# DLRM tower: six small GpSimd writes between rows of five gathers, from tile 7 on, in place of a wait for a landing

## The chip, the cores and the metric

The kernel runs on one core of a Trainium2 chip. The metric is the device time of one execution in microseconds (us), the median of several runs. The core's engines are TensorE (PE in the profile; its weight loads are PEld), VectorE (DVE), ScalarE (ACT), GpSimd (POOL) and SyncE (SP). Each has its own stream of instructions, and they are kept in step by semaphores only.

## The reference

A small recommendation model is applied to a batch of 2048 rows. For each row, 32 table lookups give 32 vectors of 16 numbers; every pair of them is multiplied and summed (496 pairs); these sums and 16 dense numbers go through three matrix layers.

```python
e = jnp.stack([tbl_0[ids[:, 0]], ..., tbl_31[ids[:, 31]]], axis=1)      # 2048 x 32 x 16
row, col = _pair_indices(32)
z = jnp.sum(e[:, row, :] * e[:, col, :], axis=2)                        # 2048 x 496
h = jnp.concatenate([z, dense_ctx], axis=1)                             # 2048 x 512
h = jnp.maximum(h @ W_top1 + b_top1, 0.0)                               # 512 x 512
h = jnp.maximum(h @ W_top2 + b_top2, 0.0)                               # 512 x 256
y = h @ W_top3                                                          # 256 x 1
```

## The kernel before

The batch is cut into 16 tiles of 128 rows, one row to a partition. Of the 32 fields, 17 have small tables (1250 or 1000 rows), which PE looks up with matmuls (`look_up`, L633). The other 15 fields have large tables and are gathered by GpSimd: one indirect DMA for each field and tile fetches 128 table rows of 64 bytes into `emb` (L367), 240 in all. The 15 fields of a tile come in three groups of 7, 5 and 3 fields.

GpSimd's program is a plain list of these gathers, tile after tile. Ahead of a group in tile t it waits until VectorE has used the group of tile t - 2 (L358). After every fifth field of a tile (`place % RUN == RUN - 1`, places 4, 9 and 14) it waits until the gather that it has just issued has landed (L373), so that the gathers go out in rows of five with a pause between rows. The last tile has no such wait: its 15 gathers, which start from 352.11 to 369.59 us, follow each other without a pause.

VectorE multiplies the groups with the fields before them as soon as a group has landed (L489, L498, L508), sums part of the pairs itself (L517), and picks the looked-up rows (L470). ScalarE copies operands into PSUM (L868, L875), the pair sums into SBUF (`copy_z`, L882), and does the layers' relus (L888, L893). PE sums the other pairs by 16 transposing matmuls for each 128 pairs (`sum_chunk`, L663; `turn`, L670, for the chunk that VectorE summed), and does the layers (L683, L692, L699). PE tells the others that it is done by a semaphore update on the last matmul of such a group (`summed`, `h1_ready`, `h2_ready`, `looked`). The engines run one or two tiles behind each other, so that a tile's layers are done while the next tile's gathers go out.

The last tile is written out by hand. Its fields are waited for in five pieces (`LAST_PIECES`, three and two fields of group 1, and then one field each of group 2). After the last field: `piece(4)`, `last_group_inside`, a sum (L517), then on PE `turn` (L670), a copy on ScalarE (L981), a quarter of layer 1 (L780), relus (L994, L607), layer 2 (L803), relus (L997, L610), layer 3 (L811), a copy (L899) and the store (L335). ScalarE's order in the last tile is `copy_group(t, 0)`, then `relu1(t - 1, 2)` and `relu1(t - 1, 3)`, then `copy_end(0, 2)`, `copy_group(t, 1)` and so on.

Of the kernel before, what the change touches and what calls it, by code (L numbers as in the profile page):

```python
# [5 lines left out]
P = 128  # L6
# [20 lines left out]
LARGE = [f for f in range(F) if f not in SMALL]  # L27
# [17 lines left out]
SUB = 16  # L45
# [7 lines left out]
GROUPS = [7, 5, 3]  # L53
GROUP_AT = [S + sum(GROUPS[:g]) for g in range(len(GROUPS) + 1)]

RUN = 5

SHIFTS = (S - 1) // 2
CIRCLES = [(GROUPS[0] - 1) // 2, (GROUPS[1] - 1) // 2, 0]
# [55 lines left out]
def dlrm_tower(nc, dense, ids, small_ids, ids_dram, tables, w1, b1, w2, b2, w3, out):  # L115
    with ExitStack() as ctx:
        def sb(name, shape, dt=F32):
            return ctx.enter_context(nc.sbuf_tensor(name, shape, dt))

        def sem(name):  # L120
            return ctx.enter_context(nc.semaphore(name))
# [16 lines left out]
        row_ten = sb("row_ten", [P, 1])  # L138
        one = sb("one", [P, 1])
        scrap = sb("scrap", [P, 1])  # L140
        cand_int = sb("cand_int", [P, SLOTS], I32)
        field_int = sb("field_int", [P, TENS, SLOTS], I32)
        place_int = sb("place_int", [P, TENS * SLOTS], I32)
# [39 lines left out]
        flat_loaded = sem("flat_loaded")  # L183
        w_loaded = sem("w_loaded")
        dense_loaded = [sem(f"dense_loaded{i}") for i in range(2)]
        ident_zeroed = sem("ident_zeroed")
        ident_ready = sem("ident_ready")
        ident_bf_ready = sem("ident_bf_ready")
# [67 lines left out]
        LAST_TILE = TILES - 1  # L256

        def steps_done(t, step):
            return STEPS * t + step + 1
# [78 lines left out]
        @block.gpsimd  # L338
        def _(pool):
            nc.gpsimd.iota(row_int[:], pattern=[[1, 1]], base=0, channel_multiplier=1).then_inc(iotas_made, 1)  # L340
            nc.gpsimd.iota(cand_int[:], pattern=[[1, SLOTS]], base=0, channel_multiplier=0).then_inc(iotas_made, 1)
            nc.gpsimd.iota(field_int[:], pattern=[[1, TENS], [0, SLOTS]], base=0, channel_multiplier=0
                           ).then_inc(iotas_made, 1)
            nc.gpsimd.iota(place_int[:], pattern=[[1, TENS * SLOTS]], base=0, channel_multiplier=0
                           ).then_inc(iotas_made, 1)
            nc.gpsimd.memset(ident[:], 0.0).then_inc(ident_zeroed, 1)
            pool.wait_ge(ident_zeroed, 1)
            nc.gpsimd.affine_select(out=ident[:], in_=ident[:], compare_op=ALU.not_equal, fill=1.0, base=0,
                                    pattern=[[-1, P]], channel_multiplier=1).then_inc(ident_ready, 1)

            pool.wait_ge(first_ids_loaded, 16)
            for t in range(TILES):
                if t == 1:
                    pool.wait_ge(ids_loaded, 16)
                for g, n in enumerate(GROUPS):
                    if t >= 2:

                        pool.wait_ge(made, steps_done(t - 2, GROUP_STEPS[g]))  # L358
                    for i in range(n):
                        f = FIELDS[GROUP_AT[g] + i]  # L360
                        at = (PLACES[g] + i) * D
                        done = landed[g][t % 2]
                        if t == LAST_TILE:
                            for k, (group, first, count) in enumerate(LAST_PIECES):
                                if group == g and first <= i < first + count:
                                    done = last_landed[k]
                        nc.gpsimd.indirect_dma_start(  # L367
                            emb[:, t, at:at + D], None, tables[f],
                            bass.IndirectOffsetOnAxis(ap=idx[:, t, f:f + 1], axis=0)
                        ).then_inc(done, 16)  # L370
                        place = GROUP_AT[g] + i - S
                        if t < LAST_TILE and place % RUN == RUN - 1:
                            pool.wait_ge(done, 16 * (t // 2 * n + i + 1))  # L373

        @block.vector
        def _(dve):
# [653 lines left out]
```

## Time and profile before

| | us |
|---|---|
| median of 3 runs | 395.4 |
| lowest and highest run | 390.53, 399.74 |
| the profiled execution | 392.31 |
| its span (first to last instruction) | 390.5 |
| POOL busy, of the span | 227.9 |
| PE busy, of the span | 301.6 |
| DVE busy, of the span | 248.0 |
| ACT busy, of the span | 145.0 |

Between the span and the profiled execution's time lie 1.8 us. Busy times of PE overlap within its pipeline. "Idle before" in the rows below is the time an engine stood still ahead of an instruction, with what ended it: a DMA, an instruction of another engine, "issue" (nothing that the profile shows), or "remote" (an update that the profile can't put to an instruction at that time).

### The profile page before, as it was taken

What the parts mean: (1) busy time and instruction counts of PE and PEld (TensorE: products, weight loads), DVE (VectorE), ACT (ScalarE), POOL (GpSimd) and SP (SyncE); (2) the same over time, 40 slices, a digit from 0 to 9 for tenths busy, and PEclk for the clock granted to TensorE, in tenths of its full rate; (3) what the DMA queues carried; (4) which work ended last, traced back from release to release, by engine and by line L of the source; (5) the groups of instructions that cost most, each with busy time, mean ns of one, the idle gap of its engine ahead of it and who ended that gap; (6) DMA issues with size and microseconds to landing.
All of it is one profiled execution on the core that took longest, in us unless ns stands there. A gap on an engine that the chain in (4) does not pass through costs nothing.

```text
span 390.5 us, 7439 instructions
## 1 busy us (share of the span) xinstructions
PE 301.6 (77%) x2748; PEld 278.9 (71%) x2748; DVE 248.0 (63%) x326; ACT 145.0 (37%) x311; POOL 227.9 (58%) x250
## 2 busy tenths in 40 slices
PE   1658697999777967977796797879679786978377
PEld 1348696888776857977785797768579776877366
DVE  6798769565956567394647739464673946556541
ACT  3982443434442424344242434424243441113012
POOL 6446655566656656665665666566566656657700
PEclk9988899899998999889899988989998898999759
DMA  6770020202020200102030110202012000000000
GB/s 140 207 236 5 8 64 6 65 6 64 8 63 5 64 6 15 53 6 63 5 64 6 24 44 6 63 6 64 6 17 51 6 6 5 7 8 6 7 3 1
DMA packets 19036, 14.51 MB, mean 37 GB/s; under 512 B 9727, under 2 KB 16461, under 8 KB 19022
## 3 DMA queue, kind: packets, MB, share of 16 engines
q1 hardware_dynamic: 10284, 11.69, 9.9%
q0 software_dynamic: 7680, 1.98, 6.5%
q10 hardware_dynamic: 1058, 0.66, 0.6%
q8 instruction: 8, 0.13, 0.2%
q14 instruction: 6, 0.05, 0.0%
HBM read 14.24 MB, written 0.08 MB: 37 GB/s over the span
## 4 chain that ended last, share of the span: by engine, by line
POOL 24%; PE 24%; issue 20%; DMA 11%; DVE 7%; another core or an unknown queue 6%; ACT 6%; SPq 1%; POOLq 0%; DVEq 0%; ACTq 0%
POOL emb L367 24%; DMA emb<-tbl,idx 10%; PE bank L663 7%; PE bank L683 6%; PE bank L645 5%; DVE emb L470 2%; PE bank L642 2%; ACT distance L844 2%; PE bank L780 1%; DVE prod L480 1%; DVE prod L489 1%; PE bank L692 1%; PE bank L699 1%; DVE mask L438 1%
## 5 line engine op out<-in xcount | busy, mean ns | idle before, releaser
L367 POOL DMA_INDIRECT emb<-tbl,idx x240 | 226.7, 945 | 141.8 <-DMA emb<-tbl,idx 80.1
L489 DVE TENSOR_TENSOR prod<-emb,bank 128x1904 f32<-128x1904 f32 (+5 forms) x51 | 94.5, 1854 | 99.3 <-DMA emb<-tbl,idx 97.3
L663 PE MATMUL bank<-ident,prod 128*128 128x128 f32 x768 | 101.9, 286 | 11.6 <-issue 4.5
L663 PEld LDWEIGHTS bank<-ident,prod 128*128 128x128 f32 x768 | 94.1, 197 | 14.3 <-issue 5.7
L683 PE MATMUL bank<-zT,w_sb 128*128 128x128 f32 x480 | 73.4, 303 | 17.7 <-ACT zT L882 16.5
L645 PE MATMUL bank<-parts,onehot 125*128 125x160 bf16 (+1 forms) x816 | 84.8, 239 | 1.8 <-issue 1.7
L683 PEld LDWEIGHTS bank<-zT,w_sb 128*128 128x128 f32 x480 | 65.9, 213 | 21.5 <-issue 19.8
L645 PEld LDWEIGHTS bank<-parts,onehot 125*128 125x128 bf16 x816 | 68.0, 104 | 1.2 <-issue 0.7
L642 PE MATMUL bank<-far_ten,named_ten 100*128 100x160 bf16 x160 | 40.9, 256 | 36.1 <-issue 26.6
L470 DVE TENSOR_REDUCE emb<-bank 128x480 f32 (+5 forms) x96 | 52.6, 583 | 10.3 <-remote 4.3
L875 ACT COPY bank<-emb 128x112 f32 (+3 forms) x32 | 7.8, 243 | 107.7 <-issue 68.4
L642 PEld LDWEIGHTS bank<-far_ten,named_ten 100*128 (+1 forms) x160 | 17.1, 107 | 42.8 <-issue 34.7
L888 ACT ACTIVATE h1T<-bank,b_sb 128x128 f32<-128x128 f32 x60 | 21.5, 362 | 57.4 <-PE bank L683 33.7
L480 DVE TENSOR_TENSOR prod<-bank,emb 128x2176 f32<-128x2176 f32 x16 | 38.7, 2418 | 5.6 <-ACT bank L868 5.5
L517 DVE TENSOR_REDUCE z_last<-prod 128x22 f32<-128x352 f32 (+3 forms) x32 | 34.8, 1087 | 2.2
L854 ACT ACTIVATE onehot<-distance,one 125x1152 bf16<-125x1152 bf16 (+1 forms) x30 | 35.7, 1194 | 0.0
L844 ACT ACTIVATE distance<-gids,minus_row 125x1152 bf16<-125x1152 f16 (+1 forms) x30 | 34.4, 1193 | 0.5 <-DMA gids<-small_ids_f 0.3
L692 PE MATMUL bank<-h1T,w_sb 128*128 128x128 f32 x240 | 31.6, 287 | 2.0 <-ACT h1T L888 1.8
L692 PEld LDWEIGHTS bank<-h1T,w_sb 128*128 128x128 f32 x240 | 29.7, 201 | 2.5 <-issue 2.4
L642 PE MATMUL bank<-far_eight,named_eight 70*128 70x128 bf16 x112 | 24.7, 221 | 7.4 <-DVE emb L470 4.7
L882 ACT COPY zT<-bank 128x512 f32<-128x512 f32 x15 | 8.8, 583 | 31.6 <-remote 30.6
L498 DVE TENSOR_TENSOR prod<-bank,emb 128x336 f32<-128x336 f32 (+1 forms) x32 | 13.2, 412 | 9.1 <-ACT emb L877 7.8
(71 smaller groups left out, 137.4 us busy)
## 6 DMA issues: line engine op xcount, KB each, us to landing
gids<-small_ids_f SPq DMA_DIRECT2D x16, 544.0 KB
emb<-tbl,idx POOLq DMA_INDIRECT x240
w_sb<-w SPq DMA_DIRECT2D x1, 1024.0 KB
w_sb<-w SPq DMA_DIRECT2D x1, 512.0 KB
tab<-tbl SPq DMA_DIRECT2D x7, 56.0 KB
tab<-tbl SPq DMA_DIRECT2D x5, 70.0 KB
tab<-tbl ACTq DMA_DIRECT2D x5, 70.0 KB
z_last<-dense SPq DMA_DIRECT2D x16, 8.0 KB
```

Of the source, the lines that this page charges most:

```text
L367: nc.gpsimd.indirect_dma_start(emb[:, t, at:at + D], None, tables[f], bass.IndirectOffsetOnAxis(ap=idx[:, t, f:f + 1], axis=0)).then_inc(d ...
L470: nc.vector.tensor_reduce(emb_at(t, SMALL_PLACE + first, n).rearrange("p a x -> p (a x)"), bank[:, from_bank, 0:width_of(r)].rearrange("p ...
L480: nc.vector.tensor_tensor(prod[:, 0:PAIR_AT[1] * D].rearrange("p (k x) -> p k x", k=SHIFTS), strided(bank[:, E_BANK, 0:S * D], [[0, SHIFTS ...
L489: return nc.vector.tensor_tensor(prod[:, at * D:(at + n * a) * D].rearrange("p (j i d) -> p j i d", j=n, d=D), strided(emb_at(t, PLACES[g] ...
L517: nc.vector.tensor_reduce(z_last[:, place, first - SUM_AT:end - SUM_AT], prod[:, first * D:end * D].rearrange("p (a d) -> p a d", d=D), AX ...
L642: nc.tensor.matmul(look, named[0:rows, bass.ts(t, P)], far[0:rows, field * w:(field + 1) * w], start=True, stop=False)
L645: mm = nc.tensor.matmul(look, onehot[:, place, i, :], parts[:, k, CAND_AT[i] * D:CAND_AT[i + 1] * D], start=False, stop=(k == PARTS - 1))
L663: mm = nc.tensor.matmul(bank[:, Z_BANK + place, c * P:(c + 1) * P], v[:, d, :], ident[:], start=(d == 0), stop=(d == D - 1), is_transpose= ...
L683: mm = nc.tensor.matmul(bank[:, H1_BANK + n % 2, 0:P], w1_sb[:, c, n * P:(n + 1) * P], zT[:, place, c, :], start=(c == 0), stop=(c == CHUN ...
L692: mm = nc.tensor.matmul(bank[:, H2_BANK, m * P:(m + 1) * P], w2_sb[:, c, m * P:(m + 1) * P], h1T[:, c, :], start=(c == 0), stop=(c == H1 / ...
L844: nc.scalar.activation(distance[:, first * P:(first + n) * P].rearrange("p (f j n) -> p f j n", f=n, n=SUB), gids[0:ROWS, place, :].rearra ...
L854: nc.scalar.activation(onehot[:, place, first:first + n, :].rearrange("p f b -> p (f b)"), distance[:, first * P:(first + n) * P], ACT.Rel ...
```

## The change

From tile 7 on (`WRITES_FROM`), GpSimd doesn't wait for the landing after places 4, 9 and 14. In its place it makes six writes (memset) of 16 columns on 128 partitions into a new tile `pace`, alternating between its two halves, and after each one it waits for that write's own semaphore update (`paced`). In the last tile the same is done after places 4 and 9, where nothing stood before; after place 14 of the last tile nothing is done. Tiles 0 to 6 keep the wait for the landing. These are 24 places where writes stand for a wait (tiles 7 to 14, three each) and 2 new ones, 156 writes in all. No other engine's program changes.

```diff
+WRITES_FROM = 7
+WRITES = 6
...
+        pace = sb("pace", [P, 2, SUB])
...
+        paced = sem("paced")
...
                         place = GROUP_AT[g] + i - S
-                        if t < LAST_TILE and place % RUN == RUN - 1:
+                        if t < WRITES_FROM and place % RUN == RUN - 1:
                             pool.wait_ge(done, 16 * (t // 2 * n + i + 1))
+                        elif place % RUN == RUN - 1 and (t, place) != (LAST_TILE, len(LARGE) - 1):
+                            row_ends = len(LARGE) // RUN * (t - WRITES_FROM) + place // RUN
+                            for k in range(WRITES):
+                                nc.gpsimd.memset(pace[:, k % 2, :], 0.0).then_inc(paced, 1)
+                                pool.wait_ge(paced, WRITES * row_ends + k + 1)
```

## Rows read from the trace of the kernel before

**Rows 1.** The page, part 5: operation, count, busy us and mean ns, idle before.
```profile
L367 POOL DMA_INDIRECT emb<-tbl,idx x240 | 226.7, 945 | 141.8 <-DMA emb<-tbl,idx 80.1 <-issue 59.1 <-DVE prod L498 1.7
L489 DVE TENSOR_TENSOR prod<-emb,bank 128x1904 f32<-128x1904 f32 (+5 forms) x51 | 94.5, 1854 | 99.3 <-DMA emb<-tbl,idx 97.3
```
**Rows 2.** POOL's waits from 175.7 to 353.2 us: us in total, times, longest.
```profile
POOL emb L367 <- DMA emb<-tbl,idx: 39.9, 24, 1.8
POOL emb L367 <- issue: 28.0, 92, 0.3
```
**Rows 3.** Timeline of POOL, one pause: start us, us, what, [idle before, its end].
```profile
256.95 0.94 POOL L367 DMA_INDIRECT emb<-tbl,idx  x1 [0.30 <-issue]
258.20 0.94 POOL L367 DMA_INDIRECT emb<-tbl,idx  x1 [0.30 <-issue]
260.81 0.94 POOL L367 DMA_INDIRECT emb<-tbl,idx  x1 [1.66 <-DMA emb<-tbl,idx]
262.05 0.94 POOL L367 DMA_INDIRECT emb<-tbl,idx  x1 [0.30 <-issue]
```
**Rows 4.** The chain that ended last, at the same pause: start us, us, what.
```profile
258.20 2.35 DMA emb<-tbl,idx
260.55 0.26 issue
```
**Rows 5.** Busy time by stretch (two middle tiles, the end): engines, granted clock, DMA share.
```profile
169.70:192.50 22.80, 18.29 (x177) 17.33 (x175) 14.40 (x17) 8.36 (x19) 14.15 (x15) 0.95 0.14 30
192.50:215.20 22.70, 18.20 (x171) 17.21 (x170) 14.15 (x17) 8.29 (x19) 14.15 (x15) 0.92 0.17 30
371.90:390.50 18.60, 14.46 (x90) 12.84 (x90) 5.38 (x11) 3.93 (x14) 0.00 (x0) 0.78 0.01 1
```
**Rows 6.** Timeline, a PE update late in a row of gathers.
```profile
311.48 0.27 PE L670 MATMUL bank<-ident,z_last 128*128 128x128 f32 x1
313.82 0.59 ACT L882 COPY zT<-bank 128x512 f32<-128x512 f32 x1 [1.81 <-remote]
314.15 0.94 POOL L367 DMA_INDIRECT emb<-tbl,idx  x1 [1.62 <-DMA emb<-tbl,idx]
```
**Rows 7.** Timeline of the last tile, ACT, DVE and PE while gathers go out.
```profile
360.39 1.95 PE L683 MATMUL bank<-zT,w_sb 128*128 128x128 f32 x16
364.40 0.23 ACT L877 COPY emb<-emb 128x48 f32<-128x48 f32 x1
364.65 0.51 DVE L498 TENSOR_TENSOR prod<-bank,emb 128x336 f32<-128x336 f32 x1 [0.48 <-issue]
367.70 0.37 PE L663 MATMUL bank<-ident,prod 128*128 128x128 f32 x1 [0.98 <-issue]
369.59 0.94 POOL L367 DMA_INDIRECT emb<-tbl,idx  x1 [0.30 <-issue]
371.93 0.45 PE L663 MATMUL bank<-ident,prod 128*128 128x128 f32 x1 [0.36 <-issue]
373.37 0.63 ACT L888 ACTIVATE h1T<-bank,b_sb 128x128 f32<-128x128 f32 x2 [8.74 <-remote]
```
**Rows 8.** Timeline of POOL at the start, the nearest rows to the new writes.
```profile
0.33 0.12 POOL L1008 MEMSET const-uint8-127<- 128x1 uint8 x1
1.36 0.20 POOL L346 MEMSET ident<- 128x128 f32 x1
1.72 0.29 POOL L348 TENSOR_SCALAR_AFFINE_SELECT ident<-ident 128x128 f32<-128x128 f32 x1 [0.16 <-POOL ident L346]
```
**Rows 9.** Timeline of DVE, two instructions that wait for the one before them.
```profile
1.64 0.15 DVE L387 TENSOR_SCALAR row_ten_int<-row_int 128x1 int32<-128x1 int32 x1
1.82 0.15 DVE L389 TENSOR_SCALAR row_ten_int<-row_ten_int 128x1 int32<-128x1 int32 x1
```
**Rows 10.** Timeline after the last landing: DVE's last work, PE's last steps.
```profile
376.38 1.18 DVE L489 TENSOR_TENSOR prod<-emb,bank 128x464 f32<-128x464 f32 x2
377.47 0.27 DVE L508 TENSOR_TENSOR prod<-emb 128x32 f32<-128x32 f32 x2
377.78 1.17 DVE L517 TENSOR_REDUCE z_last<-prod 128x61 f32<-128x976 f32 x1
384.12 0.27 PE L670 MATMUL bank<-ident,z_last 128*128 128x128 f32 x1
```

## The prediction

> **What bounds the kernel now.** I read the table of operations first, then POOL's waits, POOL's timeline, the chain that ended last, the stretches, and at last the timeline of the last tile.
>
> The table shows that GpSimd's gathers are the pace of everything. 240 gathers take 226.7 us, and GpSimd stands 141.8 us ahead of them, 80.1 us of it until a gather has landed; VectorE stands 97.3 us until a gather has landed ahead of its largest products [rows 1]. VectorE waits for gathers, and gathers wait (but for 1.7 us) for nobody but themselves. The stretches say the same of a middle tile: of 22.8 us, PE is busy in 18.3, VectorE in 14.4 and ScalarE in 8.4 [rows 5]. So a shorter stream of gathers is worth its full length until a tile comes near PE's 18.3 us.
>
> The stream has a simple form. A gather takes 0.94 us and stands 0.30 us after the one before: 1.24 to 1.25 us from start to start. At a pause it stands 1.66 us [rows 3], and this is made up of 2.35 us from the last gather's start to its landing, less its own 0.94 us, and 0.26 us from the landing to the next start [rows 4] (1.41 + 0.26 = 1.67). The 24 pauses that the change replaces sum to 39.9 us, 1.66 us each, and the longest is 1.8 [rows 2].
>
> There is a second thing that pauses do. PE ends a `turn` at 311.75, but ScalarE's copy, which waits for nothing else, starts at 313.82, just ahead of the next row of gathers at 314.15 [rows 6]. ScalarE's wait is put down to "remote": PE's update reached it about 2 us late, at the time of the landing. In the last tile, where 15 gathers go out without a pause, this becomes long. PE has done the layer 1 matmuls at 362.34; ScalarE is free at 364.63, but its relu, which needs only them, starts at 373.37, after 8.74 us. PE itself gets out single matmuls with about 1 us between them. Both end about when the last gather (369.59) has landed, near 371.9. In the same stretch VectorE answers ScalarE within 0.1 us: L877 ends at 364.63, L498 starts at 364.65 [rows 7]. So it is only what PE sends that is held while gathers go out in a long row. After 371.9 the kernel still takes 18.6 us, at a mean granted clock of 0.78 [rows 5], and the chain runs through work of PE that could have been done earlier.
>
> **The change part by part.**
>
> *The wait goes, at 24 places.* Each was 1.66 us of standing [rows 2].
>
> *Six writes come, at 26 places.* The trace has no 16-column write that waits for itself, so I build one. A 1-column write shows 0.12 us and a 128-column one 0.20 us [rows 8]; 16 columns: 0.13 us. From the end of a write to the start of the instruction that waits for it: 0.16 us on GpSimd, once [rows 8]; 0.03 us on VectorE (1.64 + 0.15 to 1.82) [rows 9]. I take the middle, 0.095 us, since the one GpSimd row is another kind of instruction after the wait. The first write ends about 0.13 us after the gather, five more take 0.13 + 0.095 each, and from the last one's end to the next gather's start I take the 0.26 us that follow a landing now [rows 4]. The new pause: 0.13 + 5 x 0.225 + 0.26 = 1.52 us. With 0.03 it is 1.19 us, with 0.16 it is 1.84 us. Queued behind these waits on GpSimd are only the gathers, and behind them VectorE's products; both are in the sum.
>
> A rule speaks against this price: the Trainium skill ("Perfetto Trace Analysis", section GPSIMD Engine Instruction) says that the reported span of a GpSimd instruction is unreliable and that instructions should be timed from start to start. What that would make of the sum is the third rival below.
>
> *The stream.* The last gather starts at 369.59. It moves by 24 x (1.52 - 1.66) = -3.4 us and by 2 x (1.52 - 0.30) = +2.4 us for the two new pauses, to 368.6. Its landing, 2.3 us later, is at 370.9. By itself the stream thus gives 1.0 us.
>
> *The end.* In the last tile rows of five stand again. Group 0 lands in the second row, ScalarE's relus follow its `copy_group` at once if PE's updates have come out at the pause, and PE does the waiting sum, layer 2 of tile 14 and half of layer 1 of tile 15 while the third row goes out (about 2 + 2 + 2 us of full-clock matmuls, the layer 1 group of 16 being 1.95 us [rows 7]). Then what follows the last landing is only what needs it: half of the pair of products (0.6), 0.27, 1.17 and some 0.1 us between them, 2.2 us in all; and from PE's `turn` at 384.12 to the end at 390.5 another 6.4 us [rows 10]. 370.9 + 2.2 + 6.4 = 379.5 us of span. Before, 18.6 us lay behind the last landing; now 8.6.
>
> The sum: the span goes from 390.5 to 379.5, the profiled execution's 392.3 to 381.3 (1.8 us lie around the span). Each 0.1 us in the pause moves this by 26 x 0.1 = 2.6 us: with 1.19 us it is 372.7, with 1.84 us 389.6. What else is near: PE is idle less in the end and could hold its clock, but if it ran at the lower level, the 6.4 us would become some 10.
>
> The median of the runs, 395.4, is 3.1 us above the profiled execution. If that is in landings that are a little later, about half of the waits for them are gone after the change (24 places of 44, the last tile having none), so I add 1.6 us and predict 383 us.
>
> **The rivals.**
>
> 1. *The stream gets no worse, but PE's hold in the last tile stays*: what PE sends comes out only at a landing with nothing behind it, and the new pauses don't let it out. For it: nothing here shows a pause without a wait for a landing. Against it: the landing falls about 1.4 us after the gather's end, inside the new pause of 1.52. Then the end keeps its 18.6 us: 370.9 + 18.6 + 1.8 = 391.3 us, no change.
>
> 2. *The pause is too short for PE.* With a pause under the 1.41 us that a landing takes after the gather's end [rows 4], the next row starts first, and what PE sends could be held over two rows, in each of the 9 tiles. In the last tile a hold cost 8.7 us [rows 7]; PE has 22.8 - 18.3 = 4.5 us to spare in a tile [rows 5]. If every tile paid the difference, 4.2 x 9 = 38 us less some 8 from the shorter pauses: about 411 us, slower. It decides below 1.41 us, where about a third of my span for the pause lies; but a hold that is ended by anything short of a full landing makes nothing of it.
>
> 3. *A write with its wait costs what the start-to-start distance shows.* From the 128-column write's start to the next instruction's start it is 0.36 us [rows 8]. Six of them and 0.26 us make a pause of 2.42 us: 381.3 + 26 x 0.90 = 404.7 us, slower. The point from which it is slower by 2% is a pause of 2.24 us (400.2 us), a write of 0.33 us. The Trainium skill's rule above, taken at its word, gives this. Against it: 0.07 us of the 0.36 are the width of that write, and GpSimd instructions that don't wait follow each other faster.
>
> 4. *GpSimd's own update is held like PE's* until the landing. Then the first write alone takes 1.41 us, and the pause is 1.41 + 5 x 0.225 + 0.26 = 2.8 us: 381.3 + 26 x 1.28 = 414.6 us. Against it: ScalarE's and VectorE's updates aren't held [rows 7].
>
> **How the numbers follow.** A difference under about 2% can hardly be told from no change here; 2% below the median is 387.5 us. The forecast with its bounds (373 to 390) has 0.62, rival 1 0.13, rival 2 0.09, rival 3 0.12, rival 4 0.04. Of the forecast's own range about one tenth lies above 387.5. Faster: 0.56. Same: 0.06 + 0.13 and some of rivals 2 and 3 in milder forms, 0.25. Slower: 0.19. The time given is the forecast's, 383 us. The range, 371 to 397, takes in the whole pause from 1.19 us on and rival 1, with a mild form of rival 3; what it leaves out is the full rivals 2 to 4.
>
> **What would show it.** POOL's timeline: the idle time plus writes between two rows, from the end of the fifth gather to the next start (1.52 us; 1.19 to 1.84), and the spacing of the writes (0.225 us). The wait list: no wait for a landing on POOL after tile 7. The last tile: the idle time ahead of ScalarE's L888 (8.74 us before, under 2 after), no PE matmuls 1 us apart, and the time from the last landing to the end (8.6 us, not 18.6). Middle tiles: PE's busy share up as the tile gets shorter (22.8 - 3 x 0.14 = 22.4 us), and ScalarE's "remote" waits ahead of L882 not longer than the 2 us of before. The prediction is wrong if the pause is above 1.8 us, or if PE's hold outlives it.

## The result and the profile after

| | before | after |
|---|---|---|
| median of 4 runs, us | 394.6 | 436.8 |
| lowest and highest, us | 390.5, 399.7 | 431.1, 447.5 |
| ratio, with its 95% interval | | 1.106 (1.088 to 1.124) |
| span of the profiled execution, us | 390.5 | 445.7 |

The change makes the kernel 10.6% slower; 383 us was forecast. The profiled execution of after was its longest run, 447.5 us, so its rows add up to some 10 us more loss than the median has.

The stream of gathers first, as in [rows 3]. The page, part 5, and POOL's timeline at two pauses of tile 7 (start us, us, what, [idle before]):

```profile
L373 POOL DMA_INDIRECT emb<-tbl,idx x240 | 226.8, 945 | 148.1 <-issue 64.3
L383 POOL MEMSET pace<- 128x16 f32 x156 | 17.8, 114 | 7.5
```
```profile
178.30 0.94 POOL L373 DMA_INDIRECT emb<-tbl,idx  x1 [0.31 <-issue]
179.25 0.97 POOL L383 MEMSET pace<- 128x16 f32 x6
180.49 0.95 POOL L373 DMA_INDIRECT emb<-tbl,idx  x1 [0.27 <-issue]
...
186.43 0.97 POOL L383 MEMSET pace<- 128x16 f32 x6
188.01 0.95 POOL L373 DMA_INDIRECT emb<-tbl,idx  x1 [0.61 <-issue]
```

A write with its wait takes 0.97 / 6 = 0.16 us, and the pause from the fifth gather's end is 0.97 + 0.27 = 1.24 us, where it was 1.66. At a tile's end, where the next gather also has to wait for VectorE's semaphore, 0.34 us come on top even if nothing is late. The gathers themselves are as long as before. So far the change does what it says, and does it better than forecast.

POOL's waits from 200 us to the last gather show what went wrong (us in total, times, longest):

```profile
POOL emb L373 <- DVE prod L500: 41.1, 6, 7.9
POOL emb L373 <- issue: 31.5, 104, 0.6
POOL emb L373 <- DVE prod L519: 3.3, 1, 3.3
```

Before, GpSimd waited 1.7 us in all for VectorE [rows 1]. Now, from tile 10 on, it stands 3.5 to 7.9 us at the start of each tile, since VectorE has not yet used the tile two back. And VectorE is late because of PE. The list of waits of the whole kernel, its longest entries on ScalarE and VectorE (us in total, times, longest):

```profile
ACT h1T L899 <- remote: 85.6, 19, 8.2
DVE emb L481 <- remote: 69.1, 23, 8.5
ACT h1T L899 <- PE bank L694: 63.9, 33, 6.8
ACT emb L871 <- DVE emb L481: 63.6, 15, 8.1
```

"Remote" is what the one wait of 8.74 us of [rows 7] and the 1.81 us of [rows 6] were put down to: an update of PE that arrives long after its matmul. In the kernel before, ScalarE's layer 1 relu (L888 there, L899 here) had 15.1 us of it in 4 waits; now 85.6 us in 19. The first line below is a group of 16 matmuls in the kernel before; the others are one such wait in the changed kernel, with PE, GpSimd and VectorE in the same stretch (lines between them left out):

```profile
309.63 2.01 PE L663 MATMUL bank<-ident,prod 128*128 128x128 f32 x16
```
```profile
282.45 0.88 PE L674 MATMUL bank<-ident,prod 128*128 128x128 f32 x3
283.86 0.61 PE L674 MATMUL bank<-ident,prod 128*128 128x128 f32 x4 [0.52 <-issue]
284.58 0.94 POOL L373 DMA_INDIRECT emb<-tbl,idx  x1 [0.30 <-issue]
285.28 0.72 PE L674 MATMUL bank<-ident,prod 128*128 128x128 f32 x5 [0.81 <-issue]
286.72 1.01 PE L674 MATMUL bank<-ident,prod 128*128 128x128 f32 x4 [0.72 <-issue]
286.82 0.37 ACT L899 ACTIVATE h1T<-bank,b_sb 128x128 f32<-128x128 f32 x1 [4.71 <-remote]
287.94 2.42 DVE L491 TENSOR_TENSOR prod<-bank,emb 128x2176 f32<-128x2176 f32 x1 [8.52 <-PE bank L681]
...
294.31 0.95 POOL L373 DMA_INDIRECT emb<-tbl,idx  x1 [7.83 <-DVE prod L500]
```

PE, which did 16 such matmuls in 2.0 us, takes 5.3 us, in bursts of three to five. The row's last gather ends at 285.52; ScalarE's relu starts 1.3 us later, and VectorE's product at 287.94, after 8.52 us in which it waited for PE. So the hold ends soon after the row, but the work behind it is late, and GpSimd, which could have gone on after a pause of 1.58 us at 287.1, stands until 294.31. Middle tiles and the stretch behind the last gather, as in [rows 5] (PE, PEld, DVE, ACT, POOL busy, granted clock, DMA share):

```profile
294.30:323.40 29.10, 23.19 (x168) 19.80 (x167) 14.27 (x17) 8.45 (x19) 16.28 (x34) 0.77 0.11 24
402.50:445.70 43.20, 38.26 (x319) 35.46 (x318) 26.79 (x32) 11.39 (x39) 0.00 (x0) 0.92 0.01 2
```

A tile takes 29.1 us, where it took 22.8. Where the work piled up is seen at the two first tiles with writes, 7 and 8, in which GpSimd isn't yet hindered:

```profile
166.10:188.00 21.90, 16.54 (x115) 13.36 (x116) 5.62 (x9) 4.63 (x12) 16.22 (x33) 0.76 0.14 31
188.00:209.90 21.90, 13.00 (x81) 11.02 (x79) 8.82 (x8) 4.79 (x10) 16.21 (x33) 0.73 0.13 32
```

PE gets out 115 and 81 matmuls in them, where it had 165 to 178 in each of tiles 7 to 13 before. These rows also show something that a reader should not pass over: the granted clock is 0.73 and 0.76 in these tiles and 0.77 to 0.85 in tiles 9 to 14, where it was 0.89 to 0.95. In the tile from 294.3 PE is busy for 23.2 us rather than 18.3 with no more matmuls; of the 6.3 us by which that tile is longer, 4.9 are PE's longer busy time and 1.4 its longer idle time. PE stood 5.4 and 8.9 us of tiles 7 and 8, in pieces, where it stood 4.5 us in each before [rows 5]. How much of the loss the lower clock makes and how much the holds by themselves, no run here separates.

The sum of the loss is exact on the span: the last gather starts at 401.07 where it started at 369.59 (+31.5), and from it to the end are 44.6 us where there were 20.9 (+23.7): 55.2 us. The first part is 44.4 us of waits for VectorE from tile 7 on, less 9.3 us that the shorter pauses give, less 3.6 us by which tile 7 started earlier in this execution, with which the change has nothing to do. The second is work of PE that had piled up: 38.3 us of the 43.2 are busy, with 319 matmuls; before, 90 matmuls were left behind 371.9 [rows 5].

### The profile page after: what moved, and what is told of

The parts are those of the page before. It is cut to its first block, busy times and chain, and to the rows that moved or that the text cites. A ratio compares the mean times of both kernels' runs of the same rounds, so it can differ in the third digit from the quotient of the medians.

```text
span 445.7 us, 7595 instructions
## 1 busy us (share of the span) xinstructions
PE 340.4 (76%) x2748; PEld 301.5 (68%) x2748; DVE 249.6 (56%) x326; ACT 145.9 (33%) x311; POOL 245.7 (55%) x406
## 4 chain that ended last, share of the span: by engine, by line
PE 58%; another core or an unknown queue 15%; issue 13%; ACT 7%; DVE 4%; SPq 1%; DMA 1%; ACTq 0%; DVEq 0%
PE bank L674 17%; PE bank L694 15%; PE bank L656 12%; PE bank L703 5%; PE bank L653 4%; ACT distance L855 3%; PE bank L710 2%; DVE emb L481 1%; DVE prod L500 1%; ACT zT L893 1%; PE bank L791 1%; ACT bank L836 1%; DVE mask L449 1%; DMA tab<-tbl 1%
## 5 line engine op out<-in xcount | busy, mean ns | idle before, releaser
L674 PE MATMUL bank<-ident,prod 128*128 128x128 f32 x768 | 113.1, 302 | 8.5 <-issue 8.0
L481 DVE TENSOR_REDUCE emb<-bank 128x480 f32 (+5 forms) x96 | 54.6, 587 | 108.7 <-remote 69.1
L694 PE MATMUL bank<-zT,w_sb 128*128 128x128 f32 x480 | 83.7, 312 | 39.6 <-ACT zT L893 19.7
L674 PEld LDWEIGHTS bank<-ident,prod 128*128 128x128 f32 x768 | 102.0, 199 | 12.8 <-issue 12.5
L656 PE MATMUL bank<-parts,onehot 125*128 125x160 bf16 (+1 forms) x816 | 95.8, 247 | 17.9 <-issue 17.8
L694 PEld LDWEIGHTS bank<-zT,w_sb 128*128 128x128 f32 x480 | 71.9, 219 | 47.9 <-issue 44.1
L656 PEld LDWEIGHTS bank<-parts,onehot 125*128 125x128 bf16 x816 | 71.0, 107 | 23.6 <-issue 22.8
L899 ACT ACTIVATE h1T<-bank,b_sb 128x128 f32<-128x128 f32 x60 | 21.7, 367 | 154.2 <-remote 85.6
L703 PE MATMUL bank<-h1T,w_sb 128*128 128x128 f32 x240 | 38.1, 314 | 7.4 <-issue 4.6
L703 PEld LDWEIGHTS bank<-h1T,w_sb 128*128 128x128 f32 x240 | 34.7, 226 | 10.1 <-issue 6.5
L871 ACT COPY emb<-emb (+1 forms) x16 | 4.8, 298 | 63.6 <-DVE emb L481 63.6
L383 POOL MEMSET pace<- 128x16 f32 x156 | 17.8, 114 | 7.5
```

Of the source, the lines that this page charges most:

```text
L481: nc.vector.tensor_reduce(emb_at(t, SMALL_PLACE + first, n).rearrange("p a x -> p (a x)"), bank[:, from_bank, 0:width_of(r)].rearrange("p ...
L656: mm = nc.tensor.matmul(look, onehot[:, place, i, :], parts[:, k, CAND_AT[i] * D:CAND_AT[i + 1] * D], start=False, stop=(k == PARTS - 1))
L674: mm = nc.tensor.matmul(bank[:, Z_BANK + place, c * P:(c + 1) * P], v[:, d, :], ident[:], start=(d == 0), stop=(d == D - 1), is_transpose= ...
L694: mm = nc.tensor.matmul(bank[:, H1_BANK + n % 2, 0:P], w1_sb[:, c, n * P:(n + 1) * P], zT[:, place, c, :], start=(c == 0), stop=(c == CHUN ...
L703: mm = nc.tensor.matmul(bank[:, H2_BANK, m * P:(m + 1) * P], w2_sb[:, c, m * P:(m + 1) * P], h1T[:, c, :], start=(c == 0), stop=(c == H1 / ...
```

## The experiments

The times are medians; the kernel before ran beside each. Three chips took part. A short diff stands with each against the changed kernel; where it is against the kernel before, the text says so.

Ahead of them one number that orders nearly all of them. From the start of one tile's first gather to the next tile's is 22.8 us in the kernel before, and 15 gathers that only follow each other take 15 x 1.248 us, so its pauses come to 4.1 us per tile, 0.27 us per gather. The same from each run's trace, from its least hindered tile of tiles 7 to 14, and from the last gather's start to the end ("tail"). The letters A, B and C are the three chips. B and C were each used at one time only, so that a difference between chips could also be one between times:

| run | chip | pause per gather, us | tail, us | median, us |
|---|---|---|---|---|
| run1w1 | B | 0.19 | 45.9 | 451.7 |
| after | not known | 0.21 | 44.6 | 436.8 |
| one1160 | A | 0.21 | 42.9 | 425.1 |
| w7 | A | 0.24 | 40.0 | 413.2 |
| w886 | B | 0.26 | 40.8 | 420.5 |
| w886_2 | C | 0.26 | 23.8 | 398.1 |
| before_again (landing waits) | C | 0.26 | 19.6 | 389.6 |
| land_all (landing waits) | A | 0.26 | 10.9 | 384.9 |
| last6 (landing waits to tile 14) | A | 0.26 | 11.8 | 385.1 |
| w8_2 | C | 0.28 | 12.2 | 386.2 |
| w8 | A | 0.28 | 10.9 | 386.7 |
| run1w2 | A | 0.34 | 10.8 | 395.3 |
| w10, w10_2 | B, C | 0.35 | 16.3, 11.9 | 395.8, 395.1 |
| run3w6 | A | 0.36 | 11.4 | 396.8 |
| both | A | 0.49 | 11.5 | 413.2 |

**Is the pause too short, or do the writes do harm?** Theory A is rival 2 as it was forecast: a hold outlives a row because the landing doesn't fall into the pause. Theory B: the writes themselves hold PE.

Eight writes (w8):

```diff
-WRITES = 6
+WRITES = 8
```

> Eight writes in place of six, nothing else. In the changed kernel six writes with their waits took 0.97 us, 0.16 us each, and the pause was 1.24 us; eight make it 1.57 us. Theory A (what PE sends is held over several rows because the pause is shorter than the 1.4 us from the gather's end to its landing): the landing falls inside the pause, no hold outlives a row, and the time is the recorded sum with a pause of 1.57 us, 381.3 + 26 x 0.05 = 383 us (380 to 390). Theory B (the writes or their semaphore updates themselves hold PE back): more writes hold it more, 437 us or over. Theory C (the length of the pause doesn't matter, only that no landing is waited for, so that the stream never stops for the queue to be seen empty): about 437 us again.

386.7 us, 0.988 of the kernel before (0.982 to 0.994): 50 us below the change, with two writes more at each place. POOL doesn't wait for VectorE at all. Its list of waits follows; the waits for a landing in it all belong to tiles 0 to 6:

```profile
POOL emb L373 <- issue: 58.6, 192, 0.3
POOL emb L373 <- DMA emb<-tbl,idx: 42.2, 21, 5.6
POOL emb L373 <- POOL pace L383: 9.7, 26, 0.6
```

Theory B falls, and C with it: no landing is waited for here either.

The landing's wait and the six writes (both):

```diff
-                        if t < WRITES_FROM and place % RUN == RUN - 1:
+                        if t < LAST_TILE and place % RUN == RUN - 1:
                             pool.wait_ge(done, 16 * (t // 2 * n + i + 1))
-                        elif place % RUN == RUN - 1 and (t, place) != ...:
+                        if t < WRITES_FROM:
+                            continue
+                        if place % RUN == RUN - 1 and (t, place) != ...:
```

> The wait for the landing is kept in tiles 7 to 14, and the six writes come behind it; the last tile has the six writes alone, as in the change. Theory A: no hold; each of the 24 pauses grows from 1.66 to about 1.41 + 0.97 + 0.27 = 2.65 us, so the stream grows by 24 us: 392.3 + 24 + 2 for the new pauses of the last tile, 410 to 418 us, with no wait of POOL for DVE. Theory B (writes hold PE): the same stream and the holds on top, over 430 us, with POOL waiting for DVE.

413.2 us, no wait for VectorE on POOL, a tail of 11.5 us. The last gather starts at 396.7, 27 us later than before: the stream's own length, and nothing else. Six writes do no harm where the pause is long.

**The last tile alone.** land_all, against the kernel before, and last6, against the change:

```diff
                         if t < LAST_TILE and place % RUN == RUN - 1:
                             pool.wait_ge(done, 16 * (t // 2 * n + i + 1))
+                        elif place == RUN - 1:
+                            pool.wait_ge(done, 16 * (t // 2 * n + i + 1))
+                        elif place == 2 * RUN - 1:
+                            pool.wait_ge(done, 48)
```
```diff
-WRITES_FROM = 7
+WRITES_FROM = 15
```

> The kernel before, with the wait for a landing after places 4 and 9 of the last tile too; no writes. It tests the term of the end alone. The recorded sum: the last gather moves back by 2 x (1.66 - 0.30) = 2.7 us, and the 18.6 us behind the last landing become 8.6: 392.3 + 2.7 - 10.0 = 385 us, with ScalarE's relu (8.74 us idle before) under 2 us. If the hold in the last tile has another cause than the long row, the end stays and the time is 395 us.

> The six writes in the last tile only, landing waits in all other tiles. Theory A: the short pause of 1.24 us doesn't release PE, so the last tile keeps most of its hold, and the time is 392.3 + 2 x 0.94 = 394 us, or a little less, if some of PE's updates slip out: 388 to 395. A theory in which a pause of any length releases PE: 384 us. In both the 45 us that the change lost aren't here, so they belong to tiles 7 to 14.

384.9 us (ratio 0.986, 0.981 to 0.992) and 385.1 us (0.985, 0.980 to 0.989), a gain of about 6 us each, where 7.3 us had been forecast for land_all. Its tail is 10.9 us where it was 20.9, the 10 us of the forecast. So pauses in the last tile do what the forecast said, and all of the change's loss comes from the pauses in tiles 7 to 14. In last6, ScalarE's relu (L899 here), which stood 8.74 us [rows 7], now follows the copy ahead of it (L888 here) at once, and PE's `turn` comes at 376.98, not 384.12 [rows 10] (timeline):

```profile
364.42 0.94 POOL L373 DMA_INDIRECT emb<-tbl,idx  x1 [0.30 <-issue]
365.42 0.23 ACT L888 COPY emb<-emb 128x48 f32<-128x48 f32 x1
365.55 0.36 ACT L899 ACTIVATE h1T<-bank,b_sb 128x128 f32<-128x128 f32 x1
...
376.98 0.33 PE L681 MATMUL bank<-ident,z_last 128*128 128x128 f32 x1
```

But last6 does this with the very pause of 1.24 us that fails in the middle, which theory A did not expect (388 to 395 us). That made theory D: what PE sends piles up while gathers go out and drains while none do, so that what counts is the pause per gather over a longer stretch. A last tile that begins drained can afford two short pauses.

**Theory A against theory D.** Seven writes (w7), and two ways to cut the pauses finer so that none is as long as a landing but the share is larger (run3w6, run1w2), and one wide write in place of six (one1160):

```diff
-WRITES = 6
+WRITES = 7                 # w7
...
+WRITE_RUN = 3              # run3w6, with WRITES = 6
+WRITE_RUN = 1              # run1w2, with WRITES = 2
...
-                        elif place % RUN == RUN - 1 and ...:
-                            row_ends = len(LARGE) // RUN * (t - WRITES_FROM) + place // RUN
+                        elif t >= WRITES_FROM and place % WRITE_RUN == WRITE_RUN - 1 and ...:
+                            row_ends = len(LARGE) // WRITE_RUN * (t - WRITES_FROM) + place // WRITE_RUN
```
```diff
-WRITES = 6
+WRITES = 1                 # one1160
...
-        pace = sb("pace", [P, 2, SUB])
+        pace = sb("pace", [P, 2, 1160])
```

> Seven writes in place of six. Pause 0.27 + 7 x 0.163 = 1.41 us, as long as the landing takes after the gather's end. Theory A (a hold ends only when nothing is outstanding, so the landing must fall inside the pause): on the edge, and some holds outlive a row: anything from 385 to 430 us, most likely 400 to 430. Theory D (what PE sends piles up while gathers go out and drains while they don't; what counts is the pause time per gather, 0.19 us over the ordinary 0.30 us in the change, 0.25 us with eight writes): between the two, 0.22 us, 384 to 410 us.

> From tile 7 on six writes after every third gather, not every fifth; the pause stays 1.24 us. Theory A: the pause is still shorter than the 1.4 us to the landing, so holds go on: 430 us or over. Theory D: pause time per gather is (1.24 - 0.30) / 3 = 0.31 us, more than with eight writes after five (0.25), so nothing outlives a row; the stream is 8 x 1.0 us longer in tiles 7 to 14 and 3.8 us in the last tile against before, and the end is 10 us shorter: 392.3 + 11.8 - 10 = 394 us (388 to 400).

> From tile 7 on two writes after every gather: no rows, a pause of 0.27 + 2 x 0.163 = 0.60 us everywhere. Theory A: no landing ever falls into a pause, the gathers never stop: the worst case, over 440 us. Theory D: 0.30 us per gather over the ordinary gap, more than with eight writes after five: no long holds, 392.3 + 8 x 0.7 + 4.2 - 10 = 392 us (386 to 400).

> One write of 1160 columns in place of six of 16. By the 128-column and the 16-column write it takes 0.115 + 1144 x 0.00074 = 0.96 us, and the pause is 1.24 us as in the change. If the length of the pause is what matters (A and D): 430 to 440 us, as the change. If the six semaphore updates and waits are what holds PE (B): 380 to 385 us.

run3w6 gave 396.8 us and run1w2 395.3 us, where theory A had 430 and 440. run1w2 pauses for 0.57 us, or 0.9 us at the start of a group (twice, from 178.7 and from 322.9 us, 1.9 us), so that but for these two places some gather is always on its way, and never waits for a landing after tile 6:

```profile
256.54 0.95 POOL L374 DMA_INDIRECT emb<-tbl,idx  x1 [0.27 <-issue]
257.49 0.30 POOL L384 MEMSET pace<- 128x16 f32 x2
258.40 0.95 POOL L374 DMA_INDIRECT emb<-tbl,idx  x1 [0.61 <-POOL pace L384]
```

Its "remote" waits on ScalarE's layer 1 relu and on VectorE's picks:

```profile
ACT h1T L900 <- remote: 19.9, 5, 5.6
DVE emb L482 <- remote: 2.3, 2, 1.5
```

85.6 and 69.1 us in the change. All of these in run1w2 lie in tiles 0 to 6, which have the waits for landings; from tile 7 on it has none, and run3w6 has 5.2 us in tile 7 and none after it. Theory A is refuted: a hold doesn't need a landing inside a pause to end.

Two things have to be kept apart here. How late PE's updates come depends on how the pauses are cut: summed over all "remote" waits of tiles 7 to 14, it is 21 us in the kernel before, 35 and 40 with eight writes, 39 in `both` with its long pauses and 116 in the change, all in rows of five, while run1w2 has 0 where w10_2, with nearly the same share in rows of five, has 33. And late updates alone cost nothing: land_all has 85.5 us of such waits in these tiles and takes 384.9 us, with PE still getting out 169 or more matmuls in each tile. What the slow runs have in common is that PE doesn't: w7 has 121 to 153 per tile, one1160 94 to 132 in tiles 7 to 10. Nor did it decide how a run stood when tile 7 began: w8 had 13.6 us of "remote" waits in tile 6, 10.6 us in each of tiles 7 and 8 and 2 to 4 us per tile from then on; w7 had 2.6 us in tile 6 and 7 to 21 us per tile from tile 7 to 13.

w7 gave 413.2 us, outside D's 384 to 410 by a little and between six and eight writes as D has it. In w7 GpSimd waits for VectorE for only 4.8 us; its last gather starts at 369.1, earlier than before, and then 40.0 us follow. The loss shows first as a backlog of PE behind the last gather, and only with less pause still as a slower stream. one1160 gave 425.1 us: one write and one update in place of six and six, at a pause of 1.36 us where 1.24 was meant (the write took 1.08 us), and the loss is there. Whether its 12 us less than the change come from the pause's form or from the chip isn't told apart.

**Where the edge lies.** Ten writes, one write per gather, and eight, eight and six writes (the last because six already make 1.58 us at a tile's end):

```diff
-WRITES = 6
+WRITES = 10                # w10
...
+WRITE_RUN = 1              # run1w1, with WRITES = 1
...
-                            row_ends = len(LARGE) // RUN * (t - WRITES_FROM) + place // RUN
-                            for k in range(WRITES):
+                            before_row = 22 * (t - WRITES_FROM) + 8 * (place // RUN)      # w886
+                            for k in range(6 if place == len(LARGE) - 1 else 8):
...
-                                pool.wait_ge(paced, WRITES * row_ends + k + 1)
+                                pool.wait_ge(paced, before_row + k + 1)
```

> Ten writes in place of eight: a pause of 1.90 us, 2.24 at a tile's end. Both theories have no hold that outlives a row here, as with eight. The recorded sum moves by 26 x 0.325 = 8.5 us against eight writes: 386.7 + 8.5 = 395 us (392 to 398). If pauses of 1.57 us still held PE back somewhat, the difference is smaller than 8.5 us.

> One write after every gather from tile 7 on (two gave 395 us, with almost no late updates of PE). The pause is 0.43 us, 0.77 at a group's start: per gather (12 x 0.13 + 3 x 0.47) / 15 = 0.20 us over the ordinary gap, about what the change has ((2 x 0.94 + 1.28) / 15 = 0.21). Theory D (pile-up and drain, the share of pause counts, not how it is cut): slow again, 415 to 445 us. If short pauses spread out were enough by themselves: the stream alone would give 395.3 - 9 x 15 x 0.163 + ... = about 376 us.

> Eight writes after places 4 and 9, six after place 14, where 0.34 us come on top anyway (the next instruction waits for VectorE too). Pauses 1.57, 1.57 and 1.58 us: per gather (1.27 + 1.27 + 1.28) / 15 = 0.255 us over the ordinary gap; seven writes everywhere had 0.247 (413 us), eight 0.28 (387 us), landings 0.27. Theory D: near the edge; if nothing is held, 386.7 - 8 x 0.33 = 384 us, the fastest of all; if the edge is above 0.255, 390 to 405 us.

These three ran on chip B, where the kernel before took 417.5 us. run1w1 gave 451.7 us: pauses spread as finely as in run1w2, at little over half the share (0.19 for 0.34), are the slowest of all, as D has it. w10 gave 395.8 us, 0.946 of the kernel before there (0.938 to 0.953; of the experiments the only one that is clearly over 2% faster than the kernel before beside it). w886 gave 420.5 us, and couldn't be judged beside w7 and w8 of chip A. So it, w8 and w10 ran again together, with the kernel before profiled beside them:

> The kernel before, profiled on this chip. On the chip of the last three runs it took 417 us, on the others 391 to 395. If this is such a slow chip, Theory D says that landings' pauses of 1.66 us (0.27 us per gather over the ordinary gap) lie under this chip's edge: many late updates of PE in tiles 7 to 14, the stream itself as long as on the other chips (last gather near 370 us), and the loss behind it. If the loss is in the gathers (longer ones, later landings), the stream is some 25 us longer. On a chip like the first: 390 to 396 us.

> Eight writes again. On a chip like the first: 387 us. On a chip where the kernel before takes 417: its 0.28 us per gather is hardly more than the landings' 0.27, so Theory D puts it near the kernel before, 400 to 420 us; a fixed edge between 1.41 and 1.57 us on every chip gives 387.

> Ten writes again (0.34 us per gather). Where the kernel before takes 417 us it took 396. On a chip like the first the sum gives 386.7 + 8.5 = 395 us as well: with this much pause the chip makes no difference.

> Eight, eight and six writes again (0.255 us per gather), this time beside eight writes on the same chip. It took 421 us where the kernel before took 417. On a chip like the first: 384 us if 0.255 is over the edge, 390 to 405 if it isn't. On a slow chip: 5 to 20 us above eight writes.

This chip (C) was like the first. before_again gave 389.6 us and so told nothing of chip B. w8_2 gave 386.2 us, 0.990 of the kernel before (0.987 to 0.994): eight writes beat the kernel before a second time, by 1.0% where it was 1.2%. w10_2 gave 395.1 us, 9.0 us over eight writes where the linear sum had 8.5. w886_2 gave 398.1 us, 12 us more than eight writes for 0.33 us less pause per tile, with the stream 3.5 us shorter and the tail 11.6 us longer. Every pause of w886 is 1.57 us or more, longer than the 1.41 us of a landing, which speaks against theory A once more. With writes in rows of five the edge is thus between 0.255 and 0.28 us per gather on chips A and C. With landing waits 0.26 was still enough there (land_all and last6, tails of 10.9 and 11.8 us); whether a landing wait does a little more than its length, or the edge lies just between 0.255 and 0.261, isn't told apart. On chip B it is higher: w886, at 0.26, had a tail of 40.8 us there and 23.8 on C. The kernel before has 0.26 to 0.27 itself, and took 417.5 us there; w10, at 0.35, took the same on both. The kernel before wasn't profiled on B, but tiles 0 to 6 of the three runs there are its program, and in tile 6 PE gets out 138, 146 and 137 matmuls (w886, run1w1, w10), where all other runs, the kernel before among them, have 165 to 198. So on B PE already falls behind with landing waits; that this makes the whole 26 us of the kernel before stays argued.

One thing no run separates. The pause per gather is the length of a tile in another form, so that D could also be worded: PE needs some 22.6 to 22.9 us for a tile, whatever the gathers do. That this is not all of it is seen in the change, which doesn't settle at such a length but at 29.1 us: once behind, PE gets slower. A kernel with less work for PE at the same pauses would tell.

## Why the prediction was wrong, step by step

**GpSimd's gathers are the pace of everything: right for the kernel before.** w10_2 against w8_2 confirms the slope: 9.0 us for two writes more at 26 places.

**The end: right, where the tiles before it aren't behind.** 10 us were to come off behind the last landing for 2.4 us of longer stream; in land_all the tail fell from 20.9 to 10.9 us for 2.7 us of waits. That its total of 384.9 us met the 385 of its forecast is luck by 1 us: the kernel before took 391.3 us beside it, not 392.3. In the changed kernel itself the tail is 44.6 us.

**The price of a write: the size was off, inside its bounds.** 0.16 us against 0.225, a pause of 1.24 against 1.52 (1.19 to 1.84 allowed). The right number was to be had from the gap of VectorE's chain [rows 9] rather than the middle. The Trainium skill's rule on timing from start to start ("Perfetto Trace Analysis", section GPSIMD Engine Instruction), which had made rival 3 with 0.36 us, holds as it is worded: six writes from start to start, 0.97 us, are what the pause is made of. It was my row for it, a 128-column write and another kind of instruction behind it, that didn't fit. A term was left out as well: where the next gather also waits for VectorE's semaphore, at a tile's end, the pause is 0.34 us longer, which is 2.7 us over eight tiles.

**"Each 0.1 us in the pause moves this by 2.6 us; with 1.19 us it is 372.7": this is the step that failed.** The line was carried down to 1.19 us as if pauses had only a price. Below some 1.5 us it turns over: eight writes (1.57 us) give 387, seven (1.41 us) 413, six (1.24 us) 437. I had read in [rows 6] and [rows 7] that pauses drain what PE sends, and used it only as a gain of the last tile. The premise behind the line, that a shorter stream is worth its full length until a tile comes near PE's 18.3 us, fell with it. At 21.9 us per tile, 3.6 us above that, PE got out 115 and 81 matmuls, not some 172; and the 18.3 us themselves held only at the granted clock of before: at 0.77 they were 23.2.

**Rival 2 named the mechanism, with a chance of 0.09, 411 us, and the wrong test.** It let a hold outlive a row if the landing misses the pause. run1w2 and run3w6 refute this: what the time follows is the share of pause, however it is cut. Its price was too small: 4.2 us for a tile, where tiles 11 to 14 took 6.3 us more (29.1 against 22.8), and nothing at the end, where the piled-up work cost 23.7 us. Its weight was too small as well. The forecast pause, 1.52 us, lay just over the threshold of 1.41 us that I gave it, with a third of my span below, so by its own terms the forecast shouldn't have had 0.62.

**Rivals 1, 3 and 4 didn't occur.** The hold in the last tile went, even with short pauses (last6); a write was cheaper than 0.36 us; and GpSimd's own updates arrive at once, or the writes would not follow each other every 0.16 us. PE's are the only ones that are late.

**What stays open**: what path PE's updates and instructions share with the gathers, why it is narrower on one chip, and how much of the loss is the lower granted clock. The traces show PE's matmuls in bursts and its updates late while gathers go out; they don't show where they are held.

## What to carry to other kernels

When a pause or a wait is shortened, ask what it does for others while it lasts, and look in the trace of before for a place without it: here the last tile, with 15 gathers in one go, showed an 8.7 us hold of PE, and that was the warning. In this kernel a stream of indirect gathers from GpSimd needs idle time in proportion to its gathers, so that PE keeps up beside it. Where a kernel of yours is built like it, measure time against that share with two or three values, for here the curve has a cliff on one side (50 us for 0.33 us of pause) and a gentle slope on the other (0.16 us per pause costs about 4 us over 26 pauses). Stay on the gentle side by a margin, since the cliff wasn't at the same place on all three chips. Of the kernels tried, pauses in the last tile alone (384.9 and 385.1 us) or eight writes in place of six (386.2 and 386.7 us) beat the kernel before by 1.0 to 1.5% on chips A and C, each by an interval that leaves out no change.

## What the hardware showed that I had not expected

- A 16-column write on GpSimd that waits for the one before takes 0.16 us from start to start (0.114 us and a gap of 0.05), and one of 1160 columns takes 1.08 us.
- PE's semaphore updates, and its matmuls, are held while gathers go out: up to 8.7 us in a row of 15, and in tiles 7 to 14 of the change, with 0.21 us of pause per gather in rows of five, 116 us over all "remote" waits. With 0.34 us per gather, after each one, there is not one such wait in these tiles. ScalarE's, VectorE's and GpSimd's own updates show nothing of the kind.
- Late updates alone don't cost time: 85.5 us of them in the same tiles of a kernel that took 384.9 us.
- When PE gets its work out in bursts, its granted clock is lower too: 0.76 and 0.73 in tiles 7 and 8 of the change, 0.95 and 0.92 in those of before.
- The kernel before took 391 to 392 us on two chips and 417 us on a third, while a program with 0.35 us of pause per gather took 395 and 396 us on two of them.
